# Convolution stage of a layer kernel: states of odd channels crossed to the other half of the partitions, in two PSUM banks, and carried sums in two halves around the next states

## The reference, cut to what matters

```python
def reference(x, cond, ...):
    h = recurrence(x, cond)              # h_t = tanh(x_t Wx + b + h_{t-1} Wh)
    x = x + conv(h)                      # the stage that is changed
    x = x + ffn(gated_scan(x, cond))     # 16 experts, top 2, and a shared one
    return x

def conv(u):                             # u: (batch, time, channel)
    dt = exp(log_dt); A = -exp(A_log)    # dt: 256 channels, A: 64 states
    K[m, t] = sum_n C_re[m, n] * exp(dt[m] * A[n] * t)
    y[b, t, m] = sum_{s <= t} K[m, t - s] * u[b, s, m]
    return y + u * D
```

## Time and profile before

| | us |
|---|---|
| median of 3 runs | 974.24 |
| lowest, highest | 974.14, 1011.77 |
| the profiled execution, its own time | 974.19 |
| its span, first to last instruction | 972.3 |
| the convolution stage in it, from the first states (388.1) to the last addition (448.5) | 60.4 |

### The profile page before, as it was taken

How to read it: one execution, slowest core, us unless ns; L and a number is a source line. 1 busy time by engine, 2 the same in 40 slices (tenths; PEclk the granted TensorE clock), 3 DMA queues, 4 the chain that set the end, 5 groups by cost and what they waited for, 6 DMA issues and landing times.

```text
span 972.3 us, 64880 instructions
## 1 busy us (share of the span) xinstructions
PE 924.3 (95%) x28864; PEld 777.5 (80%) x28864; DVE 410.7 (42%) x781; ACT 506.3 (52%) x1735; POOL 299.1 (31%) x324
## 2 busy tenths in 40 slices
PE   7999999999999999999999998999899999999993
PEld 5888888888888888996444446788899999999993
DVE  1000010100001103553899799875564646556450
ACT  2444444444444446443876587134465656566551
POOL 3111111111111110650003463760045364554545
PEclk6799999999999999999999999999999999999997
DMA  2222222221111111111001110533357666675634
GB/s 89 83 92 87 95 93 87 100 85 33 35 40 36 35 33 28 66 76 57 0 1 39 49 56 22 184 116 108 127 132 162 133 157 119 151 146 127 134 40 53
DMA packets 69161, 80.34 MB, mean 83 GB/s; under 512 B 24225, under 2 KB 53558, under 8 KB 69122
## 3 DMA queue, kind: packets, MB, share of 16 engines
q1 hardware_dynamic: 54242, 62.18, 20.3%
q0 software_dynamic: 14592, 17.10, 10.7%
q10 hardware_dynamic: 288, 0.56, 0.2%
HBM read 44.16 MB, written 33.83 MB: 80 GB/s over the span
## 4 chain that ended last, share of the span: by engine, by line
PE 81%; issue 5%; ACT 4%; POOL 4%; DVE 3%; DMA 2%; POOLq 0%; SPq 0%; ACTq 0%; DVEq 0%
PE ps L516 19%; PE ps L811 16%; PE ps L508 9%; PE ps L825 8%; PE ps L677 8%; PE ps L489 6%; PE ps L727 3%; POOL slots_in L447 2%; PE ps L577 2%; ACT tok L879 2%; PE ps L590 2%; PE ps L736 2%; PE ps L599 2%; PE ps L494 2%; DMA slots_in<-tok,arena 1%
## 5 line engine op out<-in xcount | busy, mean ns | idle before, releaser
L516 PE MATMUL ps<-tok,wh 128*32 128x8 f32 x16384 | 255.2, 180 | 12.9 <-issue 3.5
L879 ACT ACTIVATE tok<-ps 128x8 f32<-128x8 f32 x1024 | 155.9, 177 | 204.0 <-PE ps L516 201.6
L516 PEld LDWEIGHTS ps<-tok,wh 128*32 128x32 f32 x16384 | 220.0, 113 | 48.0 <-ACT tok L879 25.2
L466 POOL DMA_INDIRECT out<-arena,dest x80 | 127.9, 1599 | 99.3 <-ACT arena L1030 76.9
L489 PE MATMUL ps<-zero 128*32 128x192 bf16 x1920 | 141.1, 255 | 0.0
L418 POOL TENSOR_TENSOR big<-tok,zero 128x128 f32 x64 | 29.0, 453 | 322.0 <-ACT tok L879 322.0
L811 PE MATMUL ps<-xgT_hi,ew_hi 128*128 128x320 f32 (+1 forms) x384 | 119.5, 311 | 3.2 <-DVE spare L1275 1.6
L811 PE MATMUL ps<-xgT_hi,ew_lo 128*128 128x320 f32 (+1 forms) x384 | 119.5, 311 | 0.0
L811 PE MATMUL ps<-xgT_lo,ew_hi 128*128 128x320 f32 (+1 forms) x384 | 119.0, 310 | 0.0
L1143 DVE TENSOR_TENSOR arena<-arena,pack 128x256 f32 x32 | 13.6, 426 | 246.3 <-ACT arena L884 246.3
L1381 DVE TENSOR_TENSOR mid<-mid,ps 128x320 f32<-128x320 f32 (+1 forms) x96 | 46.6, 486 | 107.0 <-ACT mid L1048 57.5
(11 more groups left out here) (206 smaller groups left out, 1643.5 us busy)
## 6 DMA issues: line engine op xcount, KB each, us to landing
slots_in<-mid SPq DMA_DIRECT2D x16, 645.0 KB, 3.7
mid<-slots_in SPq DMA_DIRECT2D x16, 645.0 KB, 4.2
arena<-in_ex_down SPq DMA_DIRECT2D x16, 384.0 KB
arena<-in_ex_gate SPq DMA_DIRECT2D x16, 352.0 KB
arena<-in_ex_up SPq DMA_DIRECT2D x16, 352.0 KB
xst<-in_x_steps SPq DMA_DIRECT2D x66, 64.0 KB, 1.8
xtok<-in_x_tok SPq DMA_DIRECT2D x16, 256.0 KB, 2.7
mid<-k_pad SPq DMA_DIRECT2D x32, 128.0 KB, 3.1
```

The source lines that it names most:

```text
L466: pool.indirect_dma_start(out=out[:, :], out_offset=bass.IndirectOffsetOnAxis(ap=dest[:, z, t:t + 1], axis=0), in_=yo[:, z, t], in_offset= ...
L516: last = nc.tensor.matmul(sums_at(bank, t, o)[Q * j:Q * j + Q], wh[:, k, columns(j, o)], hring[:, (n - 1) % (2 * G), k], start=False, stop ...
L879: nc.scalar.activation(hring[:, n, o], sums_at(n // G, n % G, o), ACT.Tanh).then_inc(s_h[o], 1)
```

## The change

1. In `block_states` the channel c of a portion, if odd, is written to the other half of the PSUM partitions: the column half is h = k ^ (c % 2). The four places of the array are then used in turn. The 512 state columns begin in the middle of a bank and end in the middle of the next one (banks 0 and 1 for z = 0, banks 6 and 7 for z = 1), even channels first (`place_of`), so that even channels are in the one bank and odd ones in the other.
2. All that belongs to the states of odd channels is crossed with them: the decays `lam` and `d0`, `qd` and the kernel's blocks (by the order of the inputs `dt_q`, `c_q` and `masks`). The powers need the uncrossed steps, so `pack` gets a second copy `dt_s` with 128 more columns, ACT one more Exp, and POOL waits for it (`s_dtm` 4).
3. `carried` is split: first the even channels, then the odd ones, whose matmuls read half h and write the bank of the other group (k = h ^ 1). The next states stand between the two; a new semaphore `s_half` separates them.
4. The wait for the scan of portion m (`s_xc`, m + 2) now stands ahead of the first carried half, which is ahead of the states of m + 1.
5. DVE zeroes the first columns in two bank pairs: a second memset on banks 6 and 7, after the first transposes (`s_utr`).
6. `stand` writes beside the outputs in bank 2 + 2z, since bank 6 now holds states.

```diff
-        sizes = (C * B, NST, 1, P + KP, P, IT, KP * C * KP, 8, HB, RB, R + CT)
+        sizes = (C * B, NST, 1, P + KP, P, P, IT, KP * C * KP, 8, HB, RB, R + CT)
...
+        def states_at(z):
+            return psf[:, 512 * 6 * z + 256:512 * 6 * z + 768]
+        def place_of(c):
+            return CP // 2 * (c % 2) + c // 2
...
-            pool.wait_ge(s_dtm, 3)
+            pool.wait_ge(s_dtm, 4)
...
-                pool.tensor_tensor(d0[:, m % 2], lam[:, CP * m:CP * m + CP].unsqueeze(2).to_broadcast([P, CP, RB]),
-                                   resets_t.unsqueeze(1).to_broadcast([P, CP, RB]), ALU.mult).then_inc(s_d0, 1)
+                pool.tensor_tensor(d0[:, m % 2].rearrange("p (e c) r -> p e c r", e=2), lam[:, CP * m:CP * m + CP].rearrange("p (c e) -> p e c", e=2).unsqueeze(3).to_broadcast([P, 2, CP // 2, RB]),
+                                   resets_t.unsqueeze(1).unsqueeze(1).to_broadcast([P, 2, CP // 2, RB]), ALU.mult).then_inc(s_d0, 1)
...
                 for c in range(CP):
                     for k in range(C):
-                        to = ps[rows_of_half(k), z, RB * c:RB * c + RB].rearrange("p (b t) -> p b t", t=NB)[:, :, 1:NB]
+                        h, at = k ^ c % 2, RB * place_of(c)
+                        to = states_at(z)[rows_of_half(h), at:at + RB].rearrange("p (b t) -> p b t", t=NB)[:, :, 1:NB]
...
-                                                start=True, stop=True, skip_group_check=True, tile_position=(HB * k, HB * k))
+                                                start=True, stop=True, skip_group_check=True, tile_position=(HB * k, HB * h))
...
-            def carried(z):
-                for c in range(CP):
-                    for k in range(C):
+            def carried(z, crossed):
+                for c in range(crossed, CP, 2):
+                    for h in range(C):
                         for odd in range(2):
-                            last = nc.tensor.matmul(to_tokens(z, c, k, odd), qd[rows_of_half(k), CP * z + c], xc[rows_of_half(k), z, c].rearrange("p (r e) -> p r e", e=2)[:, :, odd],
...
+                            last = nc.tensor.matmul(to_tokens(z, c, h ^ crossed, odd), qd[rows_of_half(h), CP * z + c], xc[rows_of_half(h), z, place_of(c)].rearrange("p (r e) -> p r e", e=2)[:, :, odd],
...
-                last.then_inc(s_qmm, 1)
+                last.then_inc((s_half, s_qmm)[crossed], 1)
...
-                    stand()
+                    stand(z)
                     own_block(z)
+                    pe.wait_ge(s_xc, m + 2)
                     pe.wait_ge(s_pe, m + 2)
-                    pe.wait_ge(s_xc, m + 1)
                     pe.wait_ge(s_uea, 2 * m + SLOTS - 1)
-                    stand()
+                    stand(z)
+                    carried(z, 0)
                     block_states(1 - z)
-                    pe.wait_ge(s_xc, m + 2)
-                    pe.wait_ge(s_uea, 2 * m + SLOTS - 2)
-                    stand()
-                    carried(z)
+                    pe.wait_ge(s_half, m + 1)
+                    stand(z)
+                    carried(z, 1)
...
+            nc.scalar.activation(dt_s[:], dt_s[:], ACT.Exp).then_inc(s_dtm, 1)
...
-            nc.vector.memset(ps[:, 0:2].rearrange("p n (c t) -> p (n c) t", t=NB)[:, :, 0], 0.0).then_inc(s_xc, 1)
+            nc.vector.memset(ps[:, 0:2].rearrange("p n (c t) -> p (n c) t", t=NB)[:, :, 0], 0.0)
+            dve.wait_ge(s_utr, 1)
+            nc.vector.memset(ps[:, 6:8].rearrange("p n (c t) -> p (n c) t", t=NB)[:, :, 0], 0.0).then_inc(s_xc, 1)
```

More of the change, by code:

```diff
@@ L70, in build @@
         h0g = sb("h0g", [P, C, B])
-        sizes = (C * B, NST, 1, P + KP, P, IT, KP * C * KP, 8, HB, RB, R + CT)
+        sizes = (C * B, NST, 1, P + KP, P, P, IT, KP * C * KP, 8, HB, RB, R + CT)
         pack = sb("pack", [P, sum(sizes)])
-        h0r, a_bc, a_q, dt_q, c_q, d_k, masks, consts, iota_t, resets_t, rows_to = [pack[:, sum(sizes[:n]):sum(sizes[:n + 1])] for n in range(len(sizes))]
+        h0r, a_bc, a_q, dt_q, dt_s, c_q, d_k, masks, consts, iota_t, resets_t, rows_to = [pack[:, sum(sizes[:n]):sum(sizes[:n + 1])] for n in range(len(sizes))]
         h0r = h0r.rearrange("p (c b) -> p c b", c=C)
@@ L232, in build @@
         s_own = sem("s_own")
+        s_half = sem("s_half")
         s_slot_tz = [sem("s_slot_tz0"), sem("s_slot_tz1")]
@@ L240, in build @@
         block = ctx.enter_context(nc.Block())
+        psf = ps[:, :, :].rearrange("p n t -> p (n t)")
+        def states_at(z):
+            return psf[:, 512 * 6 * z + 256:512 * 6 * z + 768]
+        def place_of(c):
+            return CP // 2 * (c % 2) + c // 2
         first = ((wx, wx_d), (brow, b_rec_d))
@@ L392, in power_args @@
             def power_args(m):
-                pool.tensor_tensor(pw[:, m % 2], dt_q[:, CP * m:CP * m + CP].unsqueeze(2).to_broadcast([P, CP, NST]),
+                pool.tensor_tensor(pw[:, m % 2], dt_s[:, CP * m:CP * m + CP].unsqueeze(2).to_broadcast([P, CP, NST]),
                                    a_bc.unsqueeze(1).to_broadcast([P, CP, NST]), ALU.mult).then_inc(s_pa, 1)
@@ L1168, in carry @@
                 z = m % 2
-                nc.vector.tensor_tensor_scan(xc[:, z].rearrange("p c r -> p (c r)"), d0[:, z].rearrange("p c r -> p (c r)"), ps[:, z, :], 0.0, ALU.mult, ALU.add).then_inc(s_xc, 1)
+                nc.vector.tensor_tensor_scan(xc[:, z].rearrange("p c r -> p (c r)"), d0[:, z].rearrange("p c r -> p (c r)"), states_at(z), 0.0, ALU.mult, ALU.add).then_inc(s_xc, 1)
             def add_x(m):
@@ L1446, with crossed @@
     masks = np.zeros((P, KP, C, KP), f32)
-    masks[:, np.arange(KP), :, np.arange(KP)] = (half[:, None] == np.arange(C))[None]
+    masks[:, np.arange(KP), :, np.arange(KP)] = (half ^ np.arange(KP)[:, None] % 2)[:, :, None] == np.arange(C)
     over = np.zeros((P, KP), f32)
+    def crossed(v):
+        w = v.reshape(C, P, -1).copy()
+        w[:, 1::2] = w[::-1, 1::2]
+        return w
     steps = x.reshape(B, S // G, G // 2, 2, C, P).transpose(1, 5, 4, 3, 2, 0).reshape(S // G, P, C, G, B)
@@ L1457 @@
     tri = np.stack([np.triu(np.ones((P, P)), 1) - 1, np.ones((P, P))], 1).astype(f32)
-    pack = (rows(cond.T), np.broadcast_to(a_log, (P, NST)), np.tile(a_log, C), np.concatenate([np.repeat(dt.reshape(C, P), HB, 0), over], 1),
-            c_re.reshape(C, P, NST).transpose(0, 2, 1), d_k, masks, consts, np.broadcast_to(-np.arange(HB, dtype=f32), (P, HB)),
+    pack = (rows(cond.T), np.broadcast_to(a_log, (P, NST)), np.tile(a_log, C), np.concatenate([np.repeat(crossed(dt)[:, :, 0], HB, 0), over], 1), np.repeat(dt.reshape(C, P), HB, 0),
+            crossed(c_re).transpose(0, 2, 1), d_k, masks, consts, np.broadcast_to(-np.arange(HB, dtype=f32), (P, HB)),
             np.broadcast_to((np.arange(RB) % NB > 0).astype(f32), (P, RB)),
```

7 lines of the change are left out of this document (4 added, 3 removed).

## The result

The changed kernel takes 999.57 us (median of 4 runs, 998.66 to 1000.55); the kernel before, measured beside it, 974.52 (4 runs, lowest 974.14). The ratio is 1.0259, 95% interval 1.0238 to 1.0279: slower, where 967.0 us was forecast. One run of the four of the kernel before took 1011.77 us and is left out of the ratio; it turns out to belong to the explanation.

A forecast was written before the change was run, and what follows sets the result against it. PE's rate of getting through the convolution stage's matmul groups was taken as the bound. States -7.8, head wait +0.28, memset +0.20 and load +0.18 gave -7.15 us from 974.19: forecast 967.0 us, range 964.8 to 972.6.

The forecast's parts named there:

- The states: Convolution stage on PE: 32 state records over four places take about 0.68 us, not 1.14; 17 groups save 7.8 us.
- The portion: Convolution loop: own block, split carried sums and next states take 3.08 us per portion, where 3.54 stood.
- The head's wait for the scan: Head of the convolution loop: PE waits for the first scan before the first carried half, costing 0.28 us once.
- The second memset: DVE after the first transposes: the added memset delays the copies, costing 0.20 us (0 to 0.3).
- The load of `pack`: Program start: 128 more columns, 64 KB of DMA, before PE's first real matmul, costing 0.18 us (0 to 0.35).
- the first rival: States: streams sharing a half take turns, 94 ns per four records, 0.97 us per group; total 972.0 us; 11%.
- the second: States: a row half takes one record at a time, so groups stay at 1.14 us; total 974.9 us; 8%.
- The third rival: Convolution loop: scan or POOL becomes the bound, `block_decays` in its new pattern over 2.04 us; 971.2 us at 2.3; 5%.
- may fall otherwise than now: Granted clock, stages behind the convolution shifting: 1.5 us allowed either way, no change in the middle.
- S: Rival theory of the experiments: the changed kernel's steady portion is what the clock doesn't hold through, wherever it starts.

The follow-up runs named there:

- e8: Changed kernel with two 512-column matmuls of zeros between the first states and the loop, filling the wait for the scan: 997.62, 999.14, 1001.58 and 966.86 us.
- m1: Changed kernel with 512-column matmuls of zeros ahead of (float32) and behind (bf16) the first states, every stand a 248-column float32 matmul: 990.09 us.
- m2: Kernel before with a 512-column float32 matmul of zeros ahead of the first states and every stand a 248-column float32 matmul: 994.50 us.
- e2: Kernel before with the new order alone (carried sums split, scan's wait moved, states not crossed): 7 of 11 runs 972.93 to 979.12 us, four 1012.81 to 1015.60.
- m4: Changed kernel with two 512-column matmuls of zeros between first states and loop, the same kernel as e8 run again: 998.14 to 1002.74 us.
- e4: Kernel before with one wait more, PE waiting for the first scan ahead of the loop: 1015.58 us, ratio 1.0417.
- e5: Changed kernel with all stands 192 columns wide instead of 8: three runs at 1007.01 to 1007.11 us, one at 975.68.
- e11: Changed kernel with 512-column matmuls of zeros ahead of (float32) and behind the first states, all stands 248 columns: 1007.48, 1008.15, 1010.06 and 973.01 us.
- m3: m1 with the long stands only in every second portion: 1019.56, 1019.78, 1020.24 and 981.12 us.
- e1: Changed kernel with five 512-column matmuls of zeros ahead of the first states and two behind them: 1002.25 us, ratio 1.0275.
- e12: Kernel before with one 512-column float32 matmul of zeros ahead of the first states: 5 of 10 runs 975.48 to 977.82 us, the others 1010.48 to 1014.43.
- e3: Changed kernel with crossed states but the order of the kernel before: median 974.13 us over 10 runs, ratio 0.9991.
- e6: Kernel before with five 512-column matmuls of zeros ahead of the first states: 1010.06, 1011.13, 1015.76 and 976.45 us.
- e7: Changed kernel with both fills of e1 and the 192-column stands of e5: 1009.02 us, ratio 1.0312.
- e9: Changed kernel with a 512-column float32 matmul of zeros ahead of the first states and one 512-column bf16 behind them: 999.84 to 1003.19 us, ratio 1.0258.
- e10: e9 with 248-column stands in every second portion besides: 1001.48 to 1010.49 us, ratio 1.0302.

## Why the prediction was wrong

**What held.** Every step that could be read at full clock came out at its forecast or cheaper:

- The states: 32 records in 0.69 us, forecast 0.68, before 1.14. The portion: 3.08 us in e8's first one at full clock, forecast 3.08. In m1 against m2 the stage is 7.67 us shorter, forecast 7.8 less 0.28 for the head, which m1 with its long stands doesn't pay. A place takes its record every 58 ns also with all four places at 56 columns.
- The head's wait for the scan: 0.30 us (L617, released by L1185), forecast 0.28.
- The second memset: the copies start at 380.24 (380.13 before), the states 0.05 us later, forecast 0.20. The load of `pack`: nothing seen (the transposes start at 379.35, before 379.38), forecast 0.18, bounds 0 to 0.35.
- `block_decays` 1.06 us as before. In the changed kernel PE has no later wait in the loop, but at 5.13 us for a portion; at full clock, e8's first two portions have no wait for the scan either, and beyond them no trace shows the 3.08 us pace.

So the first rival (0.97 us per group) and the second (1.14) are refuted. With the second falls, for these 64x64 tiles, the Trainium skill's rule (TensorE: Matmul & The Clock Gate, Part 3) that loads overlap only where the row group differs: crossing leaves 16 records on each row half, and they take half the time. The third rival (POOL) is refuted by the 1.06.

**The step that failed** is the one sentence that the changes of the clock "may fall otherwise than now", priced at "1.5 us either way for this, and no change in the middle". The clock's stretches in the trace of before (up at 35.1 us, down at 693.8) were taken for fixed, and only their ends for movable. In truth the middle hung by little: in the changed kernel PE's clock falls to 0.50 at 390.2 us and gets no second chance for 88.7 us. Its cost is the 25.9 us lost from the first states to the second transposes behind the stage and the 7.15 that should have been gained ahead of that: 33 us, against the 32.6 by which 967.0 missed 999.57.

It was there to be seen. The three times of before were 974.14, 974.24 and 1011.77; the third was passed over. And the change touches exactly the place: ahead of it are 1.16 us of idle PE, which the kernel before has too; the change shortens the work behind it (0.69 for 1.14) and adds the 0.30 of wait. I priced that wait at its own length. Yet the fall doesn't need it: the clock fell 0.15 us after it began, and in e2 and m4 without it.

**What is shown and what is argued.** Shown: the fall is the loss (windows, groups 1.14 to 1.93, and the 7.67 us gained in m1 against m2 where it doesn't happen); one more stretch of idle PE at this place brings it on in the kernel before (e4, 4 of 4); neither crossing (2 of 10) nor order (4 of 11, beside 11 of 50 for the kernel before) does so every time, both together 4 of 4; the wait for the first scan isn't needed for it (m4). S in its strict form is refuted by the runs of the changed kernel's loop that held, one with the plain stands (e8) and three with wider ones (e5, e11, m3). Argued: that it is idle PE and light work at the head that add up. Filling the gap and the wait (e1) moved the fall to 399.5 us, behind the stop in the first pass, so the fill was never tried without that stop. Open: why the changed kernel falls nearly always where the kernel before falls in 11 of 50 with the same gap, how idle PE and light work are weighed (e12 held through 1.57 us), why e8 held once in eight, and whether a loop whose first pass doesn't stop would keep the clock with the plain stands. That would be the 967 us kernel; it wasn't found.

Low on both sides, the change is a gain too: a portion of the fallen kernel before is 5.97 us in e4 (410.88 to 416.85), of the changed one 5.13. 16 x 0.84 = 13 us, near the 12.2 of 1011.77 less 999.57.

## What to carry to other kernels

A stage of many small tiled matmuls can keep PE 95% busy and still be at the edge of what holds its clock; there an edit worth a few tenths of a us at its head can go with a fall that costs 25 us and more. Before trusting a sum of group times, look for one outlier among the times, take the clock row of such a run, and ask of an edit how much work PE does between its waits, not only how long it is busy. Where a loop begins, read the stops in its first pass, "issue" and those whose named releaser was done long before: added filler moves them as well.

## What the runs showed of the hardware beyond that

- At 0.50 the clock does not come back through 80 us of 64x64 matmuls, though PE shows no idle time (10.00 us busy of 10 from 391 to 401 us); it came back in the 512-column gates (at 479.0 us after a fall at 390.2). At half clock the tiled groups are 1.6 to 1.7 times as long, not twice (1.93 for 1.14; carried half 1.08 for 0.67).
- The rise at the program's start is as little fixed: in m1's profiled run it came at 51.5 us, in m2's at 35.4, and that run's first states stood 4.67 us later. It is the 993.47 among m1's times, the next ones 989.00 to 991.11.
- In a loop's first pass PE can stop for a microsecond and more while nothing of the program holds it. How long differs much from edit to edit: 0.23 us in the kernel before, under 0.1 in e3, 0.9 to 1.1 at one place in e1, e6, e7, e8, e9 and e10, up to 1.77 in e9; none in the changed kernel, e2, e4, e5 and m4, whose clock was low by then, though e1 has one of 0.65 us behind its fall. At the 13 stops of 0.6 us or more PE went on 2.3 to 3.2 us after a 16 KB packet on the instruction queue began.
- The same 1.16 us of idle PE ahead of the first states stands in profiles whose clock held (the kernel before, e3) and in others whose clock fell about 2 us behind it (the changed kernel, e2, e5). The kernel before fell in 11 of 50 runs.
